# A reordered prologue: first-layer weights and activations loaded first, second-layer operands split early, the mixing matrices formed later and copied by ScalarE

## The reference, cut to what matters

```
h   = gelu(gelu(c @ W0 + b0) @ W1 + b1)            # c: 128 x 128, one row per sample
att = softmax(h @ W2 + b2)                         # 128 x 8
m   = einsum('boi,bih->boh', att @ weight, x) + (att @ bias_k)[:, :, None]
x   = x + m @ W_base.T + b_base + low_rank(m)      # 4 of 16 experts, rank 8, softmax gate
v   = grouped_conv1d(x, weight9) + (c @ c_weight.T + bias)[:, :, None]
x   = x + v @ base_W.T + low_rank(v)               # top 2 of 28 experts, rank 8
```

## Time and profile before

| | |
|---|---|
| median of 3 runs | 390.1 us (390.02 to 390.41) |
| the profiled execution | 389.76 us, span 388.0 us |
| TensorE (PE) matmul busy | 376.9 us, 97% of the span |
| PE weight loads (PEld) | 331.3 us, 85% |
| VectorE (DVE) / ScalarE (ACT) / GpSimd (POOL) | 276.4 / 121.1 / 41.7 us |
| mean granted TensorE clock | 0.998 |

### The profile page before, as it was taken

The page is one execution under the profiler, slowest core; times in us unless marked ns, Lnnn a source line. Parts: engine busy times, 40 slices in busy tenths (PEclk is TensorE's granted clock), DMA queues, the critical chain, the costliest instruction groups (busy, mean ns, idle before and its releaser), DMA issues.

```text
span 388.0 us, 9591 instructions
## 1 busy us (share of the span) xinstructions
PE 376.9 (97%) x3183; PEld 331.3 (85%) x3183; DVE 276.4 (71%) x937; ACT 121.1 (31%) x379; POOL 41.7 (11%) x114
## 2 busy tenths in 40 slices
PE   8999899999999999999999999999999999998986
PEld 7999778888898888888988888889888888887674
DVE  6678997666776676667767767677677666776754
ACT  5266432322333223223332232233322322222211
POOL 2636720000000000000000000000000000000000
PEclk9999999999999999999999999999999999999999
DMA  6765647667777656677776656767766566676631
GB/s 216 256 182 122 161 134 194 175 154 183 162 190 182 141 149 168 153 182 162 190 179 139 157 160 155 187 162 190 180 136 160 160 159 155 139 175 156 164 80 54
DMA packets 71018, 63.05 MB, mean 163 GB/s; under 512 B 4030, under 2 KB 53502, under 8 KB 70872
## 3 DMA queue, kind: packets, MB, share of 16 engines
q1 hardware_dynamic: 70998, 62.82, 64.7%
q10 hardware_dynamic: 2, 0.00, 0.0%
HBM read 45.75 MB, written 16.91 MB: 162 GB/s over the span
## 4 chain that ended last, share of the span: by engine, by line
PE 89%; DVE 5%; DMA 3%; issue 1%; ACT 1%; SPq 1%; DVEq 0%; ACTq 0%
PE p_chy L996 14%; PE p_chy L1002 14%; PE p_chy L997 14%; PE p_u L996 9%; PE p_u L997 8%; PE p_u L1002 8%; PE p_chy L1141 8%; PE p_t L1153 3%; PE p_y L996 2%; PE p_y L1002 2%; PE p_y L997 2%; DMA win<-x_scratch 1%; DMA w_sb<-in_w 1%; PE p_y L1125 1%; PE p_chy L1077 1%
## 5 line engine op out<-in xcount | busy, mean ns | idle before, releaser
L996 PE MATMUL p_u<-w_hi,xt_hi 128*128 128x256 f32 (+1 forms) x256 | 70.5, 302 | 0.8 <-DVE w_lo L729 0.5
L997 PE MATMUL p_u<-w_lo,xt_hi 128*128 128x256 f32 (+1 forms) x256 | 68.1, 292 | 0.0
L835 DVE STREAM_TRANSPOSE c<-p_chy 128x512 f32<-128x512 f32 x32 | 22.9, 716 | 54.2 <-PE p_chy L1141 54.2
L544 ACT CAST u_hi<-p_u 128x256 fp32r<-128x256 f32 x64 | 24.9, 389 | 106.0 <-PE p_u L1002 106.0
L996 PEld LDWEIGHTS p_u<-w_hi,xt_hi 128*128 128x128 f32 x256 | 49.3, 192 | 1.5 <-issue 1.5
L593 ACT CAST g1t_hi<-p_t 112x256 fp32r<-112x256 f32 x32 | 11.9, 373 | 120.7 <-PE p_t L1153 120.7
L997 PEld LDWEIGHTS p_u<-w_lo,xt_hi 128*128 128x128 f32 x256 | 49.4, 193 | 0.0
L996 PE MATMUL p_chy<-w_hi,c_hi 128*128 128x512 f32 x124 | 49.3, 397 | 0.0
L997 PE MATMUL p_chy<-w_lo,c_hi 128*128 128x512 f32 x124 | 48.8, 394 | 0.0
L1002 PE MATMUL p_u<-w_hi,xt_lo 128*128 128x256 f32 (+1 forms) x256 | 43.0, 290 | 0.0
L1002 PEld LDWEIGHTS p_u<-w_hi,xt_lo 128*128 128x128 f32 x256 | 36.6, 190 | 0.0
(11 more groups left out here) (166 smaller groups left out, 761.9 us busy)
## 6 DMA issues: line engine op xcount, KB each, us to landing
win<-x_scratch SPq DMA_DIRECT2D x96, 256.0 KB, 4.4
x_scratch<-x SPq DMA_DIRECT2D x32, 260.0 KB, 2.1
xt_sb<-in_xt SPq DMA_DIRECT2D x32, 256.0 KB, 5.1
x_sb<-in_x SPq DMA_DIRECT2D x32, 256.0 KB, 5.1
out<-y_sb SPq DMA_DIRECT2D x32, 256.0 KB, 4.3
w_sb<-in_w SPq DMA_DIRECT2D x4, 256.0 KB, 4.9
w_sb<-in_w SPq DMA_DIRECT2D x1, 1024.0 KB, 5.9
a_sb<-in_a SPq DMA_DIRECT2D x1, 504.0 KB, 7.0
```

What stands on the lines that cost most here:

```text
L544: nc.scalar.copy(u_hi[:, t.mod(4), cols], p_u[:, banks]).then_inc(u_hi_done[half], 1)
L835: V.transpose(c1[:], p_cv).then_inc(c1_tr, 1)
L996: mm(psum, lhs_hi, rhs_hi, start=start and n == 0, stop=False)
L997: mm(psum, lhs_hi, rhs_lo, start=False, stop=False)
```

## The change

SP's list begins with the first x tile and the four quarters of `W_base`; the packed small weights (`pack`) go to ScalarE's DMA queue, ahead of the router row `rt`. The second layer's operands `a1` and `b1` are loaded before the wait for `W_base`'s last split, and `w1` right behind that wait, now ahead of the four expert loads. On ScalarE and VectorE `a1` and `b1` are split inside the prologue and the first half of `w1` too, where they stood in steps 1 and 2 (`b1`'s low part on GpSimd). On TensorE the fillers go from 5 + 18 to 8 + 2, all on unrounded ones; the W0 sums of tile 0 come first, the attention's matmuls between them; `p_mix` comes behind half a of tile 0 and the column sums of half a; half a of tile 1 moves from step 0 into the prologue. On ScalarE the late mixing matrices are copied straight from PSUM, 16 copies in four `mix_late` groups. GpSimd keeps memsets and small copies: `z_add`'s late rows go to VectorE at the end of step 2, the four rows of `win` to VectorE in step 2. The loop from step 3 on is not touched.

```diff
-            sp.dma_start(pack_sb[:], pack).then_inc(ld_pack, 16)
-            sp.dma_start(act_sb[:], active).then_inc(ld_act, 16)
-            sp.dma_start(kw_sb[:], kw).then_inc(ld_kw, 16)
             load_xt(0)
             for c in W0_ORDER:
                 load_w0(c)
+            sp.dma_start(act_sb[:], active).then_inc(ld_act, 16)
             sp.dma_start(rows_sb[:], rows_a.rearrange("p (c e n) -> p c e n", c=HC, e=E0)).then_inc(ld_rows_a, 16)
             load_xt(1)
+            sp.dma_start(kw_sb[:], kw).then_inc(ld_kw, 16)
+            sp.dma_start(a1_sb[:], a1.rearrange("p (c n) -> p c n", c=HC)).then_inc(ld_a1, 16)
             load_xt(2)
+            sp.dma_start(b1_sb[:], b1.rearrange("p (a d) -> p a d", a=2)).then_inc(ld_b1, 16)
+            sp.wait_ge(w0_lo_done, HC)
+            sp.dma_start(w_sb[:], w1.rearrange("p (c d) -> p c d", c=HC)).then_inc(ld_w1, 16)
...
-            sp.wait_ge(w0_lo_done, HC)
-            sp.dma_start(w_sb[:], w1.rearrange("p (c d) -> p c d", c=HC)).then_inc(ld_w1, 16)
-            sp.dma_start(a1_sb[:], a1.rearrange("p (c n) -> p c n", c=HC)).then_inc(ld_a1, 16)
...
+            sp.dma_start(x_sb[:, 1, :], x_v[1]).then_inc(x_loaded[1], 16)
+            sp.wait_ge(xt_lo_done, 1)
+            load_xt(4)
...
-            sp.dma_start(x_sb[:, 1, :], x_v[1]).then_inc(x_loaded[1], 16)
-            sp.wait_ge(xt_lo_done, 1)
-            load_xt(4)
...
-            b1_v = b1.rearrange("p (a d) -> p a d", a=2)
-            sp.dma_start(b1_sb[:], b1_v).then_inc(ld_b1, 16)
...
-            zero_mix(range(0, 3))
...
-            pool.tensor_copy(win[KIM:KC, 1].rearrange("k (b g) q -> k b (g q)", g=GROUPS),
-                             ident[KIM:KC, KIM:KC].unsqueeze(2).to_broadcast([BT, BT, GROUPS * NQ])).then_inc(batch_rows_done, 1)
...
-            zero_mix(range(3, NT // UNROLL))
...
-                pool.tensor_tensor(z_add[:, REST], rs0[:].unsqueeze(1).to_broadcast([P, count, Z0N]),
-                                   beta0[:, REST].unsqueeze(2).to_broadcast([P, count, Z0N]), ALU.mult).then_inc(z_rest_mul, 1)
...
+            zero_mix(range(NT // UNROLL))
...
-                        for n in range(2 * s.c - 2, 2 * s.c):
-                            for b in range(BT):
-                                pool.tensor_copy(*raw_blocks(n, b)).then_inc(mix_rest_done, 1)
...
-                    pool.tensor_tensor(b1_lo[:], b1_sb[:], b1_hi[:].bitcast(f32), ALU.subtract).then_inc(b1_lo_done, 1)
...
+            act.dma_start(pack_sb[:], pack).then_inc(ld_pack, 16)
             act.dma_start(rt_sb[:], router.rearrange("p (a e) -> p a e", a=2)).then_inc(ld_rt, 16)
...
+            def mix_late(n):
+
+                for b in range(BT):
+                    nc.scalar.copy(*mix_blocks(REST, n, b)).then_inc(mix_rest_done, 1)
...
             nc.scalar.activation(m1[:], p_mlp, ACT.Gelu, bias=pack_sb[:, C_B0:C_B0 + 1]).then_inc(m1_done, 1)
+            first, second, third = (Tile(None, t) for t in range(3))
+            w0_high(1)
             act.wait_ge(u2_mm, 1)
             nc.scalar.activation(m2[:], p_mlp, ACT.Gelu, bias=pack_sb[:, C_B1:C_B1 + 1]).then_inc(m2_done, 1)
-            act.wait_ge(am_max_done, 1)
-            nc.scalar.activation(am_exp[:], am[:], ACT.Exp, bias=am_max[:], accum_out=am_sum[:]).then_inc(am_exp_done, 1)
-            w0_high(1)
             w0_high(3)
-            first, second, third = (Tile(None, t) for t in range(3))
             xt_high(second)
             act.wait_ge(a0_done, ACT0)
             nc.scalar.copy(w0_hi[:, :, 0:Z0N], a0[:]).then_inc(a0_hi_done, 1)
+            act.wait_ge(am_max_done, 1)
+            nc.scalar.activation(am_exp[:], am[:], ACT.Exp, bias=am_max[:], accum_out=am_sum[:]).then_inc(am_exp_done, 1)
             u_high(first, "b")
-            act.wait_ge(mix_zeroed, 1)
+            act.wait_ge(ld_a1, 16)
+            nc.scalar.copy(a1_hi[:], a1_sb[:]).then_inc(a1_hi_done, 1)
+            act.wait_ge(ld_b1, 16)
+            nc.scalar.copy(b1_hi[:], b1_sb[:]).then_inc(b1_hi_done, 1)
+            u_high(first, "a")
+            xt_high(third)
+            w1_high(0)
+            act.wait_ge(mix_zeroed, NT // UNROLL)
             act.wait_ge(mix_mm, 1)
             mix_copies(FIRST, range(BT // 2))
-            u_high(first, "a")
             mix_high(first)
...
+            act.wait_ge(rsw0_mm, 1)
+            nc.scalar.copy(b0_raw[3 * L0N:3 * L0N + 3, NY:D], p_rsw0["b"][3 * L0N:3 * L0N + 3]).then_inc(rsw0b_done, 1)
...
+            u_high(second, "a")
             mix_high(second)
...
                 if at(s, 0):
                     z0_exponent(s)
-                    raw_copied(0)
-                    u_high(s + 1, "a")
+                    mix_late(0)
+                    u_high(s + 2, "b")
                     xt_high(s + 3)
-                    u_high(s + 2, "b")
                     g0t_copied(s)
-                    raw_copied(1)
                     u_high(s + 2, "a")
+                    mix_late(1)
                     xt_high(s + 4)
                     mix_high(s + 2)
...
-                    act.wait_ge(ld_a1, 16)
-                    nc.scalar.copy(a1_hi[:], a1_sb[:]).then_inc(a1_hi_done, 1)
+                    w1_high(1)
                     xt_high(s + 4)
                     u_high(s + 3, "b")
-                    w1_high(0)
+                    mix_late(2)
                     u_high(s + 3, "a")
                     g0t_copied(s)
                     mix_high(s + 2)
-                    w1_high(1)
...
-                    act.wait_ge(ld_b1, 16)
-                    nc.scalar.copy(b1_hi[:], b1_sb[:]).then_inc(b1_hi_done, 1)
+                    mix_late(3)
                     c1_high(s + -LAG)
                     u_high(s + 3, "a")
                     z0_exponent(s)
                     xt_high(s + 4)
+                    mix_high(s + 2)
                     t_exponent(s + -LAG)
                     g0t_copied(s)
-                    act.wait_ge(mix_zeroed, NT // UNROLL)
-                    mix_high(s + 2)
...
-            dve.wait_ge(mix_zeroed, 1)
-            dve.wait_ge(mix_mm, 1)
-            mix_copies(FIRST, range(BT // 2, BT))
-            u_low(first, "a")
-            mix_low(first)
             dve.wait_ge(vrow_mm, 1)
             V.tensor_copy(vrow[:], p_vrow).then_inc(vrow_done, 1)
             dve.wait_ge(zrow_mm, 1)
             V.tensor_copy(rs0[:], p_rs0).then_inc(rs0_done, 1)
+            dve.wait_ge(mix_zeroed, NT // UNROLL)
+            dve.wait_ge(mix_mm, 1)
+            mix_copies(FIRST, range(BT // 2, BT))
+            mix_low(first)
+            u_low(second, "b")
             dve.wait_ge(rs0_done, 1)
             dve.wait_ge(vrow_done, 1)
             z_rows(FIRST, 1)
-            u_low(second, "b")
...
-                    dve.wait_ge(a1_hi_done, 1)
-                    V.tensor_tensor(a1_lo[:], a1_sb[:], a1_hi[:].bitcast(f32), ALU.subtract).then_inc(a1_lo_done, 1)
+                    w1_low(0)
                     u_low(s + 3, "a")
-                    w1_low(0)
+                    w1_low(1)
                 elif at(s, 2):
                     u_low(s + 3, "b")
                     residual(s + -1)
                     c1_transposed(s + -LAG)
-                    w1_low(1)
+                    V.tensor_copy(win[KIM:KC, 1].rearrange("k (b g) q -> k b (g q)", g=GROUPS),
+                                  ident[KIM:KC, KIM:KC].unsqueeze(2).to_broadcast([BT, BT, GROUPS * NQ])).then_inc(batch_rows_done, 1)
...
-                    dve.wait_ge(z_rest_done, 1)
+                    z_rows(REST, 2)
+                    dve.wait_ge(z_add_done, 2)
...
+            def keep_busy(n):
+
+                for _ in range(n):
+                    mm(p_u[:, 0:P], ones[:], ones[:], start=True, stop=True)
+
             pe.wait_ge(ones_done, 1)
-            for _ in range(5):
-                mm(p_u[:, 0:P], ones[:], ones[:], start=True, stop=True)
-
-            pe.wait_ge(ones_r_done, 1)
-
...
-            pe.wait_ge(ld_pack, 16)
+            keep_busy(8)
             cond = pack_sb[:, C_COND:C_COND + BATCH]
-            mm(p_mlp, pack_sb[:, C_W0:C_W0 + P], cond, start=True, stop=True).then_inc(u1_mm, 1)
-
             by_batch = [slice(b * CH, (b + 1) * CH) for b in range(BT)]
-            mm(p_beta1, cond, pack_sb[:, C_CW:C_CW + CH], start=True, stop=True).then_inc(beta1_mm, 1)
-            pe.wait_ge(m1_done, 1)
-            mm(p_mlp, pack_sb[:, C_W1:C_W1 + P], m1[:], start=True, stop=True).then_inc(u2_mm, 1)
-            keep_busy(4)
-            pe.wait_ge(m2_done, 1)
-            mm(p_am, m2[:], pack_sb[:, C_W2:C_W2 + MK], start=True, stop=True).then_inc(am_mm, 1)
...
-            keep_busy(4)
             after(pe, xt_hi_done, first)
             first_chunk(0)
-            keep_busy(6)
+            pe.wait_ge(ld_pack, 16)
+            mm(p_mlp, pack_sb[:, C_W0:C_W0 + P], cond, start=True, stop=True).then_inc(u1_mm, 1)
```

(36 more changed lines are left out.)

94 lines of the change are left out of this document (29 added, 65 removed).

## The result

Over 20 executions the changed kernel took 393.7 us in the median (389.4 to 397.24), the kernel before, run beside it, 390.1 (388.14 to 391.11). The ratio is 1.0061, with a 95% interval of 1.0032 to 1.009; it counts only executions within 1.5% of the shortest, so the medians lie farther apart, 0.9%. Forecast were 387.8 and a range of 386.4 to 391.5: the wrong sign, and a median outside the range. The times form two groups. Of the 32 executions in two series 11 took 391 us or less and 20 over 392; of the 49 executions of the kernel before in these series 48 lie within 3 us of one another, and one took 515.93 for a reason that no run here shows.

What follows compares the result with a forecast made beforehand. TensorE, busy throughout from 100 to 200 us, was taken as the bound, so only an earlier start of the regular steps counts: tile 3's mixing at 49.8 for 52.09, 390.1 - 2.3 = 387.8 us, range 386.4 to 391.5.

Steps and rivals of the forecast that it cites:

- Loads and first sum: Prologue: W0's first quarter issued earlier, router row landing with `pack` at 3.65; first W0 sum at 6.95, 1.3 earlier.
- Sums of tile 0: Prologue on TensorE: half b done at 12.4, a wait of 0.7 for `a0`'s low part, half a at 16.0.
- The pace: TensorE's prologue: 2.4 GHz level from near 17.5, mixing matrices in 1.9 us, tile 0's mixing at 24.2, done 2.1 earlier.
- the marker: First mixing matmul of tile 3, from 52.09 to 49.8; its shift was taken as the shift of the end.
- Rival 1: Prologue: slow pace lasts through the mixing matrices, tile 0's mixing at 27.5 to 28.9; 391.1 to 392.5 us, chance 0.25.
- Step 0: TensorE loses about 0.9 again, as tile 0's gate on VectorE is hidden only by half b of tile 2.
- ScalarE's late copies: Sixteen late mixing copies at 0.36 us each, 1.45 for a group of four, 5.8 in all.
- Rival 2: ScalarE's copies take 0.7 each, or VectorE's list ahead of tile 1's residual is later; 389.2 us, chance 0.14.
- Windows: Tile 1, residual's end to convolution: 8.5 us for store, window loads and landing, from 40.0 to 48.5 instead of 49.91.
- Behind the marker: End of step 2: `z_add`'s late rows on VectorE, some 1.2, lie in TensorE's wait for tile 1's convolution.

Runs made afterwards that it cites:

- before_k128: Kernel before with its mixing matmuls 128 rows deep instead of 8, plus two memsets and a wait ahead of the kw load: 387.22 us, ratio 0.9932.
- tuned_8rows: Changed kernel with long fillers, router row first, early tile 1 residual, z_rows and memsets moved; against its full-row version, mixing matmuls 8 rows deep again: 387.90 us.
- fill_all: Changed kernel with longer fillers, keep_busy 14, 3 and 3 for 8, 1 and 1: 392.93 us.
- k128_fill: Changed kernel with mixing matmuls 128 rows deep and longer fillers (keep_busy 14, 3, 3): 390.34 us.
- k128_fill_rt_res: k128_fill with the router row loaded ahead of the pack and tile 1's residual ahead of W1's second low half: 390.79 us.
- tuned_z: k128_fill_rt_res with z_add's rows for the later tiles moved from the end of step 2 into step 0: 388.61 us.
- after_again: Changed kernel run once more, nothing edited, for its spread and a second profile: 394.71 us, ratio 1.0035.
- after_k128: Changed kernel with its 16 mixing matmuls 128 rows deep instead of 8, with two memsets and a wait ahead of the kw load: 391.01 us.
- before_k128_fill: before_k128 with longer fillers around W0's first two chunks, keep_busy 12, 14 and 8 for 4, 6 and 4: 390.68 us.
- tuned_few_fill: tuned_z with seven memsets moved behind att_t, but the changed kernel's own fillers (keep_busy 8, 1, 1 for 14, 3, 3), full rows kept: 389.21 us, ratio 0.9988.

## Why the prediction was wrong

**Loads and first sum** (6.95 forecast, 7.58 measured). W0's quarter was there when VectorE came to it at 6.28. Wrong was the router row: it did not land with `pack` (3.65) but at 4.27, and the copy into `win` behind it held x's cast to 5.94.

**Sums of tile 0** (half b 12.4, half a 16.0). 13.37 and 16.36: the length was right (5.79 for 5.45 in half b), the wait for `a0`'s low part was 0.22 instead of 0.7. These steps held.

**The pace: "4.9 us of such work, the breaks added, end near 17.5".** This is the step that failed. It took one trace's distance between full-row work and the rise as a price, though the prediction had said itself that no row has such breaks. The rise came at 15.6 in one execution and at 29.1 in another of the same program. In the first the pace was as good as forecast, which is chance between executions, and even so the profiled time was 389.4 where the sum has 389.76 - 2.3 = 387.46: 1.3 were lost by the marker (51.07 for 49.8) and 0.6 behind it, to the copies and the late rows told below. In the second another 5.85 were lost by tile 0's mixing and 0.95 near 56. Rival 1 describes the long execution that was profiled, and likely those at the same mean clock. It named the right mechanism and the right sign ("the fast pace comes only with the next unbroken stretch") and the right test: `p_mix` at 0.26 a matmul in the one, 0.47 in the other. Its price was too low, tile 0's mixing at 30.32 instead of 27.5 to 28.9 and 396.34 us instead of 391.1 to 392.5, and its chance of 0.25 too low. What the prediction did not see: the new opening fillers bring the fast pace early, and the idle 2.72 us take it away again near 8.7, so the sums of tile 0 begin on a falling clock. The kernel before never rose early in its profile, so it could not lose anything. The Trainium skill's rule that the prediction cited ("TensorE: Matmul & The Clock Gate", Part 1: idling brings the throttled state back) agrees with this fall. The prediction's remark that 8-row matmuls "did not speed up the pace" bore more weight than it was given: in before_k128 and tuned_8rows the edit of the rows is worth 2.6 and 1.7 us.

**Step 0** (0.9 lost). 0.28 + 0.16 were lost; better than forecast.

**ScalarE's late copies** (0.36 each, bounds 0.23 and 0.72). 0.57, 2.28 for a group instead of 1.45: a term that was mis-sized. The nearest row was of the same engine and about as many elements, but contiguous and on 3 partitions; the copies that the change adds scatter 8 by 28 elements on 32. Which of the two makes the 0.57 is not shown. Rival 2's condition came true in part: TensorE waited 0.86 for `u_lo` in step 1, and with VectorE's list behind it the residual of tile 1 ended up at 41.13 instead of 39.4.

**Windows** (8.5 from the end of the residual to the convolution). 49.87 - 41.81 = 8.06 (41.13 + 0.68), a little under the 8.1 to 8.7 that was given. `w_lo`'s halves were both at 1.22, as forecast.

**Behind the marker: "The late rows of `z_add` ... lie in that wait".** Failed. They lie behind the wait, ahead of the transposed convolution and `g1t_lo`: 0.56 of TensorE's time in the profile, 1.80 where the marker came earlier. The rule that a shift of the marker is a shift of the end holds only until VectorE's list at that point is full: from marker to end the trace has 335.9 before, 336.5 after, 338.2 with the 1.80 wait.

**`att` behind the memsets** was in no part of the prediction. The change moves eight memsets right behind the active logits, next to `att`; that costs 1.5 us of VectorE's time. In the first profile TensorE reaches `att`'s transpose after it is done and loses nothing; where the pace is fast it waits 0.83 (fill_all), 1.04 (k128_fill) or 1.65 (k128_fill_rt_res) for it, and that is the thin stretch behind which the pace fell in k128_fill and tuned_z.

## What to carry to other kernels

An operation that gets work done early is worth what the next full list lets through: look behind the marker, too, for what else was moved there. In a stretch with breaks, forecast TensorE's pace as two cases with a chance each, price the whole stretch at either, and let the unfavourable one weigh heavily when no trace shows such breaks at the fast level. Matmuls with few rows can be padded with rows of zeros: it costs two memsets and a wait ahead of the load, and as one edit with these gave 2.6 us here.

## What the runs showed of the hardware

- Rows seem to count for the clock. While matmuls with 8 of 128 rows ran without a break, TensorE fell to 1.2 GHz (fill_all at 18.1, tuned_8rows near 18.4) or did not rise (after_again, 3.78 us); in the first profile of the changed kernel they ran fast throughout (2.05 us). With 128 rows, 120 of them zeros, it rose inside them (before_k128 near 14.7, after_k128 near 22) or at their end (before_k128_fill near 18.9). That rows alone do this was not isolated.
- Unbroken work is no guarantee. In before_k128_fill TensorE was slow at 15.6 after 9 us of it; in tuned_few_fill it had work without a break over 0.22 from 12.4 and rose near 22. When the rise comes differs from execution to execution; why stays open.
- A VectorE TENSOR_SCALAR from SBUF to SBUF is held until a row of GpSimd memsets, or all but the last of them, is done (1.74 and 2.34 us for 0.23); a TENSOR_TENSOR with two SBUF operands beside them is not (1.19 for `a_lo` either way), while one beside GpSimd's copies is (0.56 for 0.19). This agrees with the Trainium skill, "SBUF — State Buffer", "SBUF: two separate sides": an operation with two SBUF inputs contends only with a GpSimd operation that reads SBUF.
- ScalarE copies 32 x 224 elements from PSUM in 0.57 us where source and target are strided; 3 x 256 contiguous ones took 0.36. Which difference makes the time was not tried.
